# A selective scan with its inputs made by a matmul instead of by ScalarE and a transpose, and two blocks of states per scan instruction in the first half

## The reference

```python
D_INNER, D_STATE, D_CONV, DT_RANK = 512, 64, 4, 64
xz = rmsnorm(x, norm_w) @ W_in.T;  xm, z = split(xz, 2)
u = silu(causal_conv4(xm) + conv_b)
dt, Bm, Cm = split(u @ W_x.T, [DT_RANK, DT_RANK + D_STATE])
delta = softplus(dt @ W_dt.T + b_dt);  A = -exp(A_log)
def step(h, inp):                      # 1024 steps, h is (512, 64) per batch
    d_t, u_t, B_t, C_t = inp
    h = exp(d_t[..., None] * A) * h + (d_t * u_t)[..., None] * B_t[:, None, :]
    return h, einsum('bdn,bn->bd', h, C_t)
y = (scan(step) + u * Dp) * silu(z)
out = y @ W_out.T + x
```

## Time and profile before

| | |
|---|---|
| Time, median of 3 runs | 2889.66 us (2880.05 to 2891.95) |
| Profiled execution, its own time | 2885.97 us |
| Span of that execution | 2884.1 us |
| Mean granted clock of TensorE | 0.934 of full speed |
| Busy share of the span | PE 82%, DVE 68%, ACT 63%, POOL 46% |

### The profile page before, as it was taken

One profiled execution on the slowest core, in us unless ns is written; L12 is line 12 of the kernel. 1 busy time (PEld: TensorE's weight loads), 2 busy tenths in 40 slices (PEclk: granted clock), 3 DMA queues, 4 the chain that ended last, 5 costly groups with the idle time before them and its releaser, 6 DMA issues. The chain is left out here.

```text
span 2884.1 us, 38743 instructions
## 1 busy us (share of the span) xinstructions
PE 2360.6 (82%) x12450; PEld 1196.7 (41%) x12451; DVE 1956.8 (68%) x1790; ACT 1802.8 (63%) x2808; POOL 1314.1 (46%) x493
## 2 busy tenths in 40 slices
PE   7588888888877888888888867788778689969799
PEld 2244444444334444444443423223322555536444
DVE  7699999999768999999993465923841312225520
ACT  5799999999568999999993324065036311112331
POOL 2099998999606999899991111000000210020000
PEclk9799999999988999999998788899989799979999
DMA  2410001000124000100000220010001510020000
GB/s 94 112 50 26 29 26 41 26 29 25 46 62 103 30 25 25 41 29 26 25 19 17 61 89 1 1 35 26 1 23 35 225 37 22 22 79 1 9 0 30
DMA packets 61705, 115.65 MB, mean 40 GB/s; under 512 B 13587, under 2 KB 21907, under 8 KB 60576
## 3 DMA queue, kind: packets, MB, share of 16 engines
q1 hardware_dynamic: 52992, 103.20, 11.1%
q0 software_dynamic: 8608, 11.05, 1.3%
HBM read 86.39 MB, written 27.53 MB: 39 GB/s over the span
## 5 line engine op out<-in xcount | busy, mean ns | idle before, releaser
L1129 POOL TENSOR_TENSOR hs<-hs,c_bc 128x2048 f32<-128x2048 f32 x256 | 1166.3, 4556 | 65.8 <-DVE hs L1180 50.4
L1180 DVE TENSOR_TENSOR_SCAN hs<-decays,carry,ps 128x512 f32<-128x512 f32 x512 | 620.9, 1268 | 10.9 <-PE ps L1207 9.4
L1180 DVE TENSOR_TENSOR_SCAN hs<-decays,ps 128x512 f32<-128x512 f32 x512 | 610.8, 1215 | 25.2 <-PE ps L1207 6.8
L1215 PE MATMUL ps<-hs,sel 128*64 128x512 f32 x2048 | 499.9, 609 | 14.1 <-POOL hs L1129 13.8
L1207 PE MATMUL ps<-ident,dbu_even 128*128 128x128 f32 x2048 | 295.1, 283 | 93.7 <-DVE hs L1180 65.9
L1207 PE MATMUL ps<-ident,dbu_odd 128*128 128x128 f32 x2048 | 294.5, 283 | 92.2 <-DVE hs L1180 61.4
L1143 ACT ACTIVATE decays<-delta_far,A 128x512 f32<-128x512 f32 x512 | 357.4, 711 | 12.0 <-DVE hs L1180 11.8
L1143 ACT ACTIVATE decays<-delta_near,A 128x512 f32<-128x512 f32 x512 | 356.0, 706 | 2.0 <-DVE hs L1180 2.0
L1151 ACT ACTIVATE dbu_odd<-du_turned,b_turned 128x512 f32<-128x512 f32 x512 | 356.6, 708 | 0.0
L1151 ACT ACTIVATE dbu_even<-du_turned,b_turned 128x512 f32<-128x512 f32 x496 | 345.3, 708 | 0.0
L1207 PEld LDWEIGHTS ps<-ident,dbu_odd 128*128 128x128 f32 x2048 | 220.8, 142 | 241.9 <-DVE hs L1180 188.2
(11 more groups left out here) (284 smaller groups left out, 2655.5 us busy)
## 6 DMA issues: line engine op xcount, KB each, us to landing
c_bc<-c_rows SPq DMA_DIRECT2D x256, 128.0 KB, 2.8
o_rows<-osb SPq DMA_DIRECT2D x32, 256.0 KB
u_rows<-u SPq DMA_DIRECT2D x4, 1024.0 KB, 4.5
d_rows<-delta SPq DMA_DIRECT2D x4, 1024.0 KB, 4.2
delta_near<-d_rows SPq DMA_DIRECT2D x4, 1024.0 KB, 9.6
hs<-u_rows SPq DMA_DIRECT2D x4, 1024.0 KB, 6.7
delta_far<-d_rows SPq DMA_DIRECT2D x4, 1024.0 KB, 12.5
w_down<-in_expert_proj SPq DMA_DIRECT2D x1, 4096.0 KB, 36.4
```

The source lines that it names most:

```text
L1129: pool.tensor_tensor(x, x, spread(c_bc[:, g, :], 4), ALU.mult).then_inc(weighed.sem, 1)
L1180: dve.tensor_tensor_scan(hs[:, quad % RING, n, :], decays[:, s % RING, :], ps[:, DBU + s % RING, :], carry[:, at(i * GB, g), blk] if q els ...
L1215: mm = pe.matmul(ps[lo:lo + DB, ACC + quad % 2 * 2 + j // 2, :], k.sel2[:, :], hs[:, quad % RING, j, :], start=False, stop=False, skip_gro ...
```

## The change

`scan_inputs` and `scan` no longer make du x B on ACT. ACT makes diagonal matrices of B: for each group, 2 states x 4 chunks of 128 time steps, each the identity scaled per partition by B (`b_diag`, 128x128). PE multiplies the turned du by such a diagonal, which scales by B and turns in one product: per unit 2 states x 4 chunks = 8 matmuls, 64 channels x 128 steps each, one state into partitions 0 to 63 and the other into 64 to 127.

In the first half, DVE scans two units by one instruction of 1024 columns over two neighbouring banks; the decay of the second unit's first column is set to 0 once (`opened`), and ACT makes that unit's decays from column 1 on, so that the state starts anew. ACT may be 8 decays ahead of DVE (AHEAD) instead of 4. The last states of a quad are copied to `carry` by ACT (`keep_last`) instead of by POOL.

Input and weights have memory of their own, so that store, reload and the wait for it go away. The core of the diff:

```diff
-        room = [k.sb(n, [P, QT, NB, PAIR, DB], ctx=ctx) for n in ("dbu_even", "dbu_odd")]
-        flat = [r[:, :, :, :, :].rearrange("p a b c d -> p (a b c d)") for r in room]
+        flat = [k.sb(n, [P, QT * DI * PAIR], ctx=ctx)[:, :] for n in ("xn_room", "scan_weights")]
+        b_diag = k.sb("b_diag", [P, 2, PAIR, QT, P], ctx=ctx)
...
-            if b:
-                pe.wait_ge(again.sem, again.at(16 * 4))
...
-            def first_products():
-
-                if b == 0:
-                    act.wait_ge(xn_stored.sem, xn_stored.at(16))
-                for t in range(QT):
-                    take("du", 0, t, du_t[:, t, :], ACT.Copy)
-                for t in range(QT):
-                    act.wait_ge(taken.sem, taken.at(take_no["du", 0, t]))
-                    for n in range(PAIR):
-                        act.activation(first_dbu[:, t, :, n, :], du_t[:, t, :].rearrange("p (b d) -> p b d", d=DB),
-                                       ACT.Copy, scale=b_t[:, t, n:n + 1]).then_inc(prefilled.sem, 1)
+            def first_diagonals():
+
+                act.wait_ge(taken.sem, taken.at(take_no["B", 0, 0]))
+                for n in range(PAIR):
+                    for t in range(QT):
+                        act.activation(b_diag[:, 0, n, t, :], k.ident[:], ACT.Copy, scale=b_t[:, t, n:n + 1])\
+                           .then_inc(prefilled.sem, 1)
...
-            if b == 0:
-                both = flat[0].rearrange("p (c n) -> p c n", c=C)
-                sp.dma_start(k.xn_rows, both[:, :, T:2 * T]).then_inc(xn_stored.sem, 16)
...
-    RING = 4
+    RING, AHEAD = 4, 8
...
-    decays = k.sb(f"decays{b}", [P, RING, W], ctx=ctx)
+    decays = k.sb(f"decays{b}", [P, AHEAD, W], ctx=ctx)
...
-            if reload:
-                sp.wait_ge(turned.sem, turned.at(1 + CPB * LOOPS * UNITS))
-                for to, source in reload:
-                    sp.dma_start(to, source).then_inc(again.sem, 16)
...
-                    pool.wait_ge(scanned.sem, count(scanned, q, i, UNITS, RING + 4 * quad + 4))
                     if q == 0:
-                        pool.tensor_copy(carry[:, at(i * GB, g), half * 4:half * 4 + 4],
-                                         x[:, :, W - 1:W].rearrange("p c o -> p o c")).then_inc(carried.sem, 1)
                         pool.wait_ge(carried.sem, count(carried, q, i, QUADS, quad + 1))
+                    else:
+                        pool.wait_ge(scanned.sem, count(scanned, q, i, UNITS, AHEAD + 4 * quad + 4))
...
+            def keep_last(i, quad):
+                g, half = divmod(quad, 2)
+                act.activation(carry[:, at(i * GB, g), half * 4:half * 4 + 4],
+                               hs[:, quad % RING, :, W - 1:W].rearrange("p c o -> p o c"), ACT.Copy)\
+                   .then_inc(carried.sem, 1)
...
-                    act.activation(decays[:, s % RING, :], (far if q else near)[:, blk, :], ACT.Exp,
+                    joined = 0 if q else s % 2
+                    act.activation(decays[:, s % AHEAD, joined:W], (far if q else near)[:, blk, joined:W], ACT.Exp,
                                    scale=A[:, at(i * GB, g), blk]).then_inc(decay.sem, 1)
+                    if q == 0 and s % 4 == 3:
+                        if s > 3:
+                            act.wait_ge(scanned.sem, count(scanned, q, i, UNITS, AHEAD + s - 3))
+                            keep_last(i, s // 4 - 1)
...
-                            act.activation(dbu[0], dbu[1], ACT.Copy, scale=dbu[2]).then_inc(made.sem, 1)
+                            act.activation(made_of[0], k.ident[:], ACT.Copy, scale=made_of[1]).then_inc(made.sem, 1)
...
+            dve.memset(decays[:, :, 0:1], 0.0).then_inc(opened.sem, 1)
+            dve.sem_inc(scanned.sem, AHEAD)
...
+                    if q == 0 and s % 2 == 0:
+                        continue
                     dve.wait_ge(decay.sem, count(decay, q, i, UNITS, s + 1))
                     dve.wait_ge(turned.sem, count(turned, q, i, UNITS, 1 + s + 1))
...
+                    else:
+                        place, bank = s % AHEAD - 1, DBU + s % RING - 1
+                        dve.tensor_tensor_scan(hs[:, quad % RING, n - 1:n + 1, :].rearrange("p c n -> p (c n)"),
+                                               decays[:, place:place + 2, :].rearrange("p c n -> p (c n)"),
+                                               ps[:, bank:bank + 2, :].rearrange("p c n -> p (c n)"),
+                                               0.0, ALU.mult, ALU.add).then_inc(scanned.sem, 2)
...
-                pe.wait_ge(scanned.sem, count(scanned, q, i, UNITS, s + 1))
+                pe.wait_ge(scanned.sem, count(scanned, q, i, UNITS, AHEAD - RING + s + 1))
                 for t in range(QT):
-                    mm = pe.transpose(ps[:, DBU + s % RING, t * P:(t + 1) * P],
-                                      room[g % 2][:, t, blk, :, :].rearrange("p n d -> p (n d)"), k.ident[:])
+                    for n in range(PAIR):
+                        mm = pe.matmul(ps[n * DB:(n + 1) * DB, DBU + s % RING, t * P:(t + 1) * P],
+                                       du_t[:, q * QT + t, blk * DB:(blk + 1) * DB], b_diag[:, g % 2, n, t, :],
+                                       start=True, stop=True)
                 mm.then_inc(turned.sem, 1)
```

More of the change, by code:

```diff
@@ L716, in mamba_batch @@
     near = k.sb("delta_near", [P, NB, W], ctx=ctx)
-    if b == 0:
-        xn = flat[0].rearrange("p (c n) -> p c n", c=C)[:, :, 0:T]
-    else:
-        xn = flat[0][:, 0:C * T].rearrange("p (c n) -> p c n", c=C)
+    xn = flat[0].rearrange("p (c n) -> p c n", c=C)[:, :, b * T:(b + 1) * T]
     with ExitStack() as c2:
[L722 to L726, removed]
+        scan_inputs(k, b, xn, w, vec, A, diag, zs, du_t, b_t, near, b_diag, c2)
     with ExitStack() as c2:
-        scan(k, b, A, room, du_t, b_t, near, diag, zs, reload, c2)
+        scan(k, b, A, du_t, b_t, b_diag, near, diag, zs, c2)
     tiles = []
@@ L735, in mamba_batch, with scan_inputs @@
     project(k, tiles)
-def scan_inputs(k, b, flat, xn, w, vec, A, diag, zs, du_t, b_t, near, first_dbu, ctx):
+def scan_inputs(k, b, xn, w, vec, A, diag, zs, du_t, b_t, near, b_diag, ctx):
     nc, ps = k.nc, k.ps
@@ L923, in _ @@
             take_z(1)
[L924 removed]
+            first_diagonals()
+            take_du()
         @block.vector
@@ L1030, in spread_delta, with scan @@
         sp.dma_start(to[n * DB:(n + 1) * DB, :, :], rows[:, :, h * W:(h + 1) * W]).then_inc(here.sem, 16)
-def scan(k, b, A, room, du_t, b_t, near, diag, zs, reload, ctx):
+def scan(k, b, A, du_t, b_t, b_diag, near, diag, zs, ctx):
     nc, ps = k.nc, k.ps
@@ L1073, in all_bodies, with diagonal @@
             body(q, LOOPS - 1)
-    def product(q, i, g, n, t):
+    def diagonal(q, i, g, n, t):
         if isinstance(i, int) and (i, g) == (LOOPS - 1, GB - 1):
@@ L1135, in _ @@
             act.sem_inc(made.sem, 1)
+            def keep_last(i, quad):
[3 more added lines that the diff above has]
+                   .then_inc(carried.sem, 1)
             def body(q, i):
+                first = isinstance(i, int) and i == 0
                 for s in range(UNITS):
                     g, blk = divmod(s, NB)
+                    if first and q == 0 and s == 0:
+                        act.wait_ge(opened.sem, opened.at(1))
                     if q and isinstance(i, int) and (i, s) == (0, 0):
@@ L1142, in body @@
                     act.wait_ge(scanned.sem, count(scanned, q, i, UNITS, s + 1))
-                    act.activation(decays[:, s % RING, :], (far if q else near)[:, blk, :], ACT.Exp,
+                    joined = 0 if q else s % 2
+                    act.activation(decays[:, s % AHEAD, joined:W], (far if q else near)[:, blk, joined:W], ACT.Exp,
                                    scale=A[:, at(i * GB, g), blk]).then_inc(decay.sem, 1)
+                    if q == 0 and s % 4 == 3:
+                        if s > 3:
+                            act.wait_ge(scanned.sem, count(scanned, q, i, UNITS, AHEAD + s - 3))
+                            keep_last(i, s // 4 - 1)
+                        elif not first:
+                            act.wait_ge(scanned.sem, count(scanned, q, i, UNITS, AHEAD))
+                            keep_last(i - 1, QUADS - 1)
+                    if first and q == 1 and s == 3:
+                        act.wait_ge(scanned.sem, count(scanned, q, i, UNITS, AHEAD))
+                        keep_last(LOOPS - 1, QUADS - 1)
                     for place in range(MADE_AT[blk - 1] if blk else 0, MADE_AT[blk]):
                         n, t = divmod(place, QT)
-                        dbu = product(q, i, g, n, t)
-                        if dbu:
+                        made_of = diagonal(q, i, g, n, t)
+                        if made_of:
                             if place == 0:
                                 act.wait_ge(turned.sem, count(turned, q, i, UNITS, 1 + g * NB))
```

(13 more changed lines are left out.)

27 lines of the change are left out of this document (9 added, 18 removed).

## The result

| | before | changed |
|---|---|---|
| Time, median of 4 runs each | 2887.18 us | 2978.8 us (2974.29 to 2981.45) |
| Ratio, 95% interval | 1 | 1.0315 [1.0297, 1.0333] |
| Profiled execution, span | 2884.1 us | 2976.3 us |
| Its own time | 2885.97 us | 2978.06 us |

The kernel became 3.2% slower, by 92 us, where 2985 us, 97 us more than before, was forecast.

A forecast was written before the change was run, and what follows sets the result against it. It took ACT, DVE and POOL as level at 4.90 us a quad, with PE the bound after the change at 5.24: +87 us, plus +10 for edges, forecast 2985 us; range 2950 to 3095.

The forecast's parts named there:

- PE becomes the bound: In the scans, PE's quad becomes 5.24 us, over today's 4.90; 0.34 us over 256 quads gives +87 us.
- PE's slack, 0.76 us a quad: In the kernel before, PE has 4.14 us of work in a 4.90 us quad, so only 0.76 is free.
- The slot, 0.110 us: In the new product, two tiles streaming one 128-column record each take 0.110 us, between 0.1075 and 0.123.
- The sums, 1.72 us without the change of tiles: A quad's sums on PE are 4 slots of 0.43 us, 1.72; the 0.15 us tile change is left out.
- Weights hidden: PE's 64-column weight loads, 0.061 us each, hide behind streaming; rival of unhidden loads: slot 0.171, 3482 us, chance 0.06.
- The queue feeds 64 short records a quad: PE's queue keeps up; rival that it can't: 0.057 us a record, 3016 us, slower feed to 3100, chance 0.06.
- POOL's copy on ACT, cost nothing: In the scans, POOL loses its copy, needs about 4.60 us a quad, under 5.24; waiting for ACT's copy costs nothing.
- The pairs worth nothing while PE bounds: In the first half, DVE's paired scans take 4.44 to 4.88 us a quad, under 5.24, so pairing saves nothing.
- Banks, "by a hair": Second pair's banks come free at 3.4 us, needed at 3.48: no stall; stall rival 3095 us, chance 0.07.
- Edges, +10 us: Per batch: start about +2 us, skip's products about +5, sums behind the last scan -2; +5 a batch.
- The sum: 87 + 10 = 97 us, own time 2983 us; forecast median 2985 us, 3.3% slower.
- The memory of their own brings nothing: Between the scans, memory no longer shared gains nothing: PE's own queue releases the next batch, DVE's chain to du covers slices.

The follow-up runs named there:

- experiment 1: Changed kernel with each product of B streaming 64 of its 128 columns, half of du x B left out: 2819.18 us, ratio 0.9787 to the kernel before.
- experiment 4: Changed kernel with the copy to `carry` back on POOL, ACT's `keep_last` taken out: 2977.91 us, ratio 1.0332 to the kernel before.
- the mixture with single scans: Changed kernel with diagonals for even-numbered groups only, slices and transposes for odd ones, one unit per scan instruction: 2841.69 us, ratio 0.9846.

## Why the prediction was right

- **PE becomes the bound.** Right. PE 280.00 of 280, quad 5.21 us against 5.24 forecast; 256 x 0.31 = 79 us for 87.
- **PE's slack, 0.76 us a quad.** Misread, without harm to the sum. It comes from busy time; by starts the slack was 4.90 - 3.77 = 1.13 us, and the change puts 1.44 on it. The sum went by 5.24 less 4.90, in which the quad of today's PE has no part, and the overshoot of 0.31 is the same either way.
- **The slot, 0.110 us.** 0.109. That columns set the price, taken from the sums in the same tiles, is what experiment 1 confirmed (0.058 at half the columns). The prices of short runs, 0.123 and 0.14 from the earlier trace rows, don't hold in a long one.
- **The sums, 1.72 us without the change of tiles.** Right to the digit: 302.88 to 304.60. The 0.15 us that the prediction left out (1.87 less 1.72) went away with the transposes, as assumed. The Trainium skill (TensorEngine Tiling (Array Packing), Key Properties) says that a change of tiling mode drains TensorE, and this agrees.
- **Weights hidden.** Right: loads are busy 218 of 280 us, beside a PE that does not stop.
- **The queue feeds 64 short records a quad.** Right. 0.109 us for two is 0.055 us a record, below the 0.057 that bounded the estimate. The Trainium skill (TensorE: Matmul & The Clock Gate, Wait — 56ns, not 53.3ns?) gives about 62 ns per matmul with hardware decode off; no such limit shows here, and with half the columns a record took 0.029 us. No trace says which decode was on.
- **ACT.** A diagonal costs 0.29 to 0.30 us from start to start (its row says 389 ns, and the next instruction starts before it ends). 208 of 280 us for 3.81 / 5.21 x 280 = 205.
- **POOL's copy on ACT, cost nothing.** Right (experiment 4).
- **The pairs worth nothing while PE bounds.** Right, and short of the truth: they are worth next to nothing at all. One pair takes 2.26 us and two without a wait between them 4.46 (the first two rows here, from the changed kernel), so 2.20 from start to start. Eleven single scans without a wait between them take 12.31 us in the mixture with single scans (third row), and one takes 1.22 (1215 ns in the earlier trace rows), so (12.31 - 1.22) / 10 = 1.11 from start to start and 2.22 for two:

```profile
298.42 2.26 DVE L1185 TENSOR_TENSOR_SCAN hs<-decays,ps 128x1024 f32<-128x1024 f32 x1
...
301.42 4.46 DVE L1185 TENSOR_TENSOR_SCAN hs<-decays,ps 128x1024 f32<-128x1024 f32 x2 [0.75 <-PE ps L1214]
```

```profile
298.96 12.31 DVE L1181 TENSOR_TENSOR_SCAN hs<-decays,ps 128x512 f32<-128x512 f32 x11
```

- **Banks, "by a hair".** Right for these sizes, with more room than forecast: DVE is named for 4.7 us in front of all products. The pairs start 2.20 us apart and not 2.44, so that the two from 301.42 on end at 305.88, and PE needs the banks of the second pair half way through its products, at 304.60 + 3.49 / 2 = 306.35, almost 0.5 us later.
- **Edges, +10 us.** They were 13, 92 less 79. The skips came to 5.2 us in batch 0 and 4.3 in batch 1, 9.5 for the 10 forecast. The start is 1.3 us later (137.24 for 135.90), where about 2 was forecast, but that it is near is luck: DVE waited for ACT's second decay and not for PE's second unit. PE was not slow there. From 134 to 136 us it did 34 records at a granted clock of 1.00, its 2.4 GHz, where the kernel before had 0.50, its 1.2 GHz, and its first 32 slots took 3.71 us, 0.11 each and not the 0.22 forecast (before, then two rows of the changed kernel):

```profile
134.00:136.00 2.00, 1.79 (x9) 1.82 (x10) 0.10 (x1) 1.99 (x3) 0.00 (x0) 0.50 0.40 113
```

```profile
134.00:136.00 2.00, 1.86 (x34) 1.89 (x36) 0.00 (x0) 1.99 (x3) 0.00 (x0) 1.00 0.42 124
```

```profile
134.14 3.71 PE L1214 MATMUL ps<-b_diag,du_turned 128*64 128x128 f32 x64 [1.50 <-DVEq L1154]
```

The stretch from POOL's last start in batch 0 to DVE's first scan in batch 1 also grew, from 112.1 us (768.23 to 880.36) to 115.3 (814.03 to 929.28). That was not forecast, and no run took it apart. From PE's first product to POOL's last start, the scan of batch 0 takes 679.9 us (134.14 to 814.03) for the 683 forecast.
- **The sum.** It has a slip of 2 us. 2885.97 + 97 is the own time of the profiled execution, and with the 3.7 for the median it makes 2987 and not 2985. 2978.8 was measured.
- **The memory of their own brings nothing.** No gain can be seen where the reload had stood: the stretch between the scans grew by 3.1 us. That the reload by itself costs nothing was read from the traces and wasn't tried by a run.

## What to carry to other kernels

A change that takes work from one of several level engines has to be paid with the slack of the engine that gets it: here 1.1 us a quad left ACT and 1.44 came to PE, which had 1.13 to give, and the overshoot of 0.31 us times 256 was 79 of the 92 us lost. Read the slack from the starts of instructions that didn't wait: busy time put it at 0.76. Price each engine per period, and where the two ways of a step load different engines, alternate them in a ratio that leaves both under the next bound, which gave 1.5% (with single scans; 1.1% with pairs) where all of the one lost 3.2%. A long instruction in place of two short ones is worth what lies between the starts of the short ones beyond their columns, and on DVE that was under 1%.

## What the runs showed of the hardware that was not expected

- A scan of 1024 columns over two PSUM banks saves almost no start-up: 2.20 us from start to start, against 2 x 1.11 for two of 512 from 0.0 without waits. The rows' durations (2274 ns and 1215 ns) suggest a gain of 6% that the starts don't show.
- Float32 products of 128 columns in two tiles of 64 columns run for whole halves at 0.109 us for two records, each with its own weight load, with no pause at semaphore waits that were already met. With 64 columns two records take 0.058 us.
